# Second input ahead of the layer weights, and a reordered last stage, in a two-part attention and FFN kernel

## The chip, the cores and the metric

The kernel runs on one core of one Trainium2 chip. The metric is device time in microseconds (us), the median of three runs. The engines are named as in the profile: PE (TensorE; PEld its weight load), DVE (VectorE), ACT (ScalarE), POOL (GpSimd), SP (SyncE, whose queue issues every DMA here).

## What is computed

Eight sequences of 512 tokens with 256 features, all f32. Cut to its core:

```
xn = layernorm(x)                                  # over the features
s  = causal softmax attention(rotate(xn wq'), rotate(xn wk'), xn wv')
g  = xn
for l in range(2):                                 # two layers
    g = g + local_attention(shift(g) wqkv[l]) wo[l]        # 8 heads of 64, window 128
    h = layernorm(shift(g)) * ln_g[l] + ln_b[l]
    a, gate = split(h w1[l] + b1[l])                       # hidden width 682
    g = g + (a * gelu(gate)) w2[l] + b2[l]
out = x + s * silu(g)
```

`shift` delays the second half of the features by one token.

## The kernel before

Features lie on the partitions for the products, tokens for the softmax. Each f32 product is made of three fp32r products (high by high, high by low, low by high), so a value is split into a high part on ACT and a low part (the difference) on DVE or POOL.

**First block** (`attention_block`). It computes `xn` and `s`, batch by batch, in a software pipeline written out by hand: `step(0)` has only the front (transposes of x, projections, rotation), steps 1 to 7 have the front of one batch and the back (scores, softmax, values) of the one before, and step 8 only the back. Each engine has its own program of these steps, in order, tied by semaphores. SP first issues x of batch 0 (L289), the identity matrix and the three weights (one semaphore `w_in` for all, L293), the rotation tables and the mask (semaphore `c_in`, three DMAs, L294 to L296), and then everything that the second block wants for layer 0: `load_small` (31 small DMAs, L124 to L142), `wo` (L116), `w2` (L119, L120) and `wqkv` (L104). Only then comes `step(0)`, with x of batch 1 (L307), which waits until the normalized x of batch 0 is made (semaphore `xn`), for both use the one buffer `x_in`. POOL first multiplies the layers' tables by the scales of q and k (L324, semaphore `small`), then makes the rotation's second products (`t2`, L335 and L336). DVE waits for `c_in` at its start, before `statistics(0)` (L456). PE waits for all of `w_in` before it turns the weights (L568). In `step(0)` ACT runs `high`, `copy_x`, `proj(0)` (L348), `norm(1)` (it needs the statistics of batch 1), `proj(1)` and so on; DVE runs `low`, `statistics(1)`, `moments(1)`, `rotate(0)` (its sum is L485), `normal(1)` (L468), `rotate(1)` to `rotate(3)`.

**Second block** (`layers_block`). A pipeline over 16 (layer, batch) pairs: attention of pair i with the FFN of pair i-1. The last step, 16, has no attention (`if not attn`): it runs the FFN of the last batch, and the end of the kernel for all batches. The end of a batch is: PE turns a half of its features back to tokens (`turned_back(n)`, L1339, n = 2 b + half), ACT takes the silu of it (`silu(n)`, L921), and DVE multiplies by s and adds x (`combine(b)`, L1083 and L1085), after x and s of that batch have landed in `xs` (L786, 16 DMAs of 512 KB). SP then writes the batch out. Two PSUM banks take turns for n, so `turned_back(n)` waits for `silu(n-2)`. The FFN of the last batch goes: mean (L1241), difference (L1123), square on ACT (L945), sum of the squares on DVE (`sum_squares`, L1128), variance on PE (L1245), Ln and Exp on ACT (L949, L951), normalization on DVE (L1134), high part on ACT (`high_f`, L955), low part on DVE (L1145), first FFN product (`hidden`, L1260, 66 products), gelu on ACT (L903), `gated` (L1058) and `u_low` (L1067) on DVE, second FFN product (`down`, L1270, 18 products for each half of the features), `add_ffn` on DVE (L1073), and then the turns, silus and combines of batch 7.

ACT holds one table of functions at a time; `preload_act_table_set` loads one by name (L964 and L972 in this step).

Of the kernel before, what the change touches and what calls it, by code (L numbers as in the profile page):

```python
# [7 lines left out]
ALU = mybir.AluOpType  # L8
# [6 lines left out]
P = 128  # L15
B, N, D = 8, 512, 256
# [27 lines left out]
def at(ap, i):  # L44

    return ap[:, bass.ds(i, 1)]
# [158 lines left out]
def attention_block(nc, outer, io, W, xT, ident, identb, ones, epsc):  # L205
# [4 lines left out]
    with ctx:  # L210
# [6 lines left out]
        def sem(name):  # L217
# [41 lines left out]
        w_bank = (ring[0], ring[1], psT)  # L259
        qkT_bank = (psT, psP[0])  # L260

        names = ("id_in id_bf consts w_in c_in w_tr w_hi w_lo x_in0 bn agg lnv rstd xn xT_ps xT_hi xT_sb xT_lo "
                 "proj_ps proj_sb t2_done t1_done rot_done qkT_ps qkT_sb s_ps m_bias exp_done "
                 "rinv_done pT_ps pT_sb o_ps o_sb out_dma").split()
        S = {n: sem(n) for n in names}
# [7 lines left out]
        def pipeline(e, step):  # L273

            step(0, True, False)
            with e.Fori(1, B - 1) as i:
                step(i, True, True)
            step(B - 1, True, True)
            step(B, False, True)
# [7 lines left out]
        @block.sync  # L287
        def _(sp):
            sp.dma_start(x_in[:, :, :], x_v[0]).then_inc(S["x_in0"], 16)  # L289
            for j, w in enumerate(("wq", "wk", "wv")):  # L290
                if j == 0:
                    sp.dma_start(ident[:, :], io["ident"]).then_inc(S["id_in"], 16)
                sp.dma_start(wraw[:, KD * j:KD * (j + 1), :], io[w].rearrange("(k p) d -> p k d", p=P)).then_inc(S["w_in"], 16)  # L293
            sp.dma_start(cosT[:, :, :], io["acos"]).then_inc(S["c_in"], 16)  # L294
            sp.dma_start(sinT[:, :, :], io["asin"]).then_inc(S["c_in"], 16)
            sp.dma_start(maskT[:, :], io["amask"]).then_inc(S["c_in"], 16)  # L296
            W.load_small(sp, scl, scls)
            W.load_wo(sp, 0)
            sp.wait_ge(WS["w2pad"], 1)
            W.load_w2(sp, 0)  # L300
            sp.wait_ge(S["w_tr"], 3)
            W.load_wqkv(sp, 0, stage_q)

            def step(i, front, back):
                if has_next(i, front):
                    ge(sp, S["xn"], i + 1)
                    sp.dma_start(at(x_in[:, :, :].unsqueeze(1), 0), x_v[bass.ds(i + 1, 1)].rearrange("b p t d -> p b t d")).then_inc(S["x_in0"], 16)  # L307
                if back:
                    ge(sp, S["o_sb"], TT * i)
                    sp.dma_start(s_v[bass.ds(i - 1, 1)].rearrange("b p t d -> p b t d"), O[:, :, :].unsqueeze(1)).then_inc(S["out_dma"], 16)  # L310
                if isinstance(i, int) and i == B - 1:
                    W.load_w1(sp, 0, stage1)
            pipeline(sp, step)
            sp.wait_ge(S["out_dma"], 16 * (B + 1))

        @block.gpsimd
        def _(pool):
            pool.wait_ge(S["c_in"], 48)

            pool.wait_ge(WS["small"], W.SMALL)  # L320
            for l in range(LAYERS):
                for tab, s in ((W.cosT, scl), (W.sinT, scls)):
                    rows = tab[:, l].rearrange("p t j d -> p t (j d)")
                    pool.tensor_tensor(rows, rows, s[:, l].rearrange("p j d -> p (j d)").unsqueeze(1).broadcast_to([P, TT, 2 * DH]), ALU.mult).then_inc(WS["tabs"], 1)  # L324

            def step(i, front, back):
                if front:
                    for t in range(TT):

                        ge(pool, S["proj_sb"], TILES * i + t + 1)  # L330
                        ge(pool, S["rot_done"], TT * i + t - 1)
                        src = raw[:, t % 2, :].rearrange("p (q c s) -> p q c s", q=2, s=2)
                        dst = t2[:, t % 2, :].rearrange("p (q c s) -> p q c s", q=2, s=2)
                        tab = sinT[:, t, :].rearrange("p (c s) -> p c s", s=2).unsqueeze(1).broadcast_to([P, 2, D // 2, 2])
                        pool.tensor_tensor(dst[:, :, :, 0], src[:, :, :, 1], tab[:, :, :, 0], ALU.mult).then_inc(S["t2_done"], 1)  # L335
                        pool.tensor_tensor(dst[:, :, :, 1], src[:, :, :, 0], tab[:, :, :, 1], ALU.mult).then_inc(S["t2_done"], 1)  # L336
            pipeline(pool, step)

        @block.scalar
# [104 lines left out]
        def _(dve):  # L444
# [3 lines left out]
            dve.memset(W.b1raw[:, :, :], 0.0).then_inc(WS["b1pad"], 1)  # L448
            dve.memset(W.w2_raw[:, HFULL, :], 0.0).then_inc(WS["w2pad"], 1)
            dve.memset(spare[:, :], 0.0).then_inc(S["out_dma"], 16)  # L450
            dve.wait_ge(S["c_in"], 48)

            def statistics(i):
                ge(dve, S["x_in0"], 16 * (i + 1))
# [98 lines left out]
            for j in range(3):  # L553
                dve.wait_ge(S["w_hi"], j + 1)
                part = slice(j * D, (j + 1) * D)
                dve.scalar_tensor_tensor(out=wlo[:, :, part], in0=w_bank[j][:, :].rearrange("p (k o) -> p k o", k=KD), scalar=w_scale[j],
                                         in1=whi[:, :, part].bitcast(F32), op0=ALU.mult, op1=ALU.subtract).then_inc(S["w_lo"], 1)
            pipeline(dve, step)

        @block.tensor  # L560
        def _(pe):

            pe.wait_ge(S["id_in"], 16)
            pe.wait_ge(S["w_in"], 48)
            for j in range(3):
                for k in range(KD):
                    for o in range(KD):
                        last = pe.transpose(w_bank[j][:, k * D + o * P:k * D + (o + 1) * P],  # L568
                                            wraw[:, KD * j + o, k * P:(k + 1) * P], ident[:, :])
                last.then_inc(S["w_tr"], 1)  # L570
# [102 lines left out]
def layers_block(nc, outer, io, W, xT, ident, identb, ones, epsc):  # L673
# [3 lines left out]
    with ctx, stack:  # L677
# [184 lines left out]
        def _(act):  # L862
# [77 lines left out]
            def step(i, la, lf, last=False):  # L940
# [6 lines left out]
                def inverse_deviation():  # L947
                    ge(act, S["var_ps"], i)
                    act.activation(rstdF[:, :], psF[:, N:2 * N], ACT.Ln, bias=epsc[:, 0:1]).then_inc(S["lnF_done"], 1)  # L949
                    ge(act, S["lnF_done"], i)  # L950
                    act.activation(psF[:, 0:N], rstdF[:, :], ACT.Exp, scale=-0.5).then_inc(S["rstdF_done"], 1)  # L951
# [5 lines left out]
                if not attn:  # L957

                    act.preload_act_table_set(SILU)
                    for n in range(9):  # L960
                        silu(n)
                    square()
                    silu(9)
                    act.preload_act_table_set(NLE)  # L964
                    inverse_deviation()
                    high_f()
                    for j in range(HT):
                        gelu(i, j, lf, attn)
                        if j:
                            u_high(i, j - 1, attn)  # L970
                    u_high(i, HT - 1, attn)
                    act.preload_act_table_set(SILU)  # L972
                    for n in range(10, 2 * B):
                        silu(n)
                    return
                if attn:
# [46 lines left out]
        def _(dve):  # L1023
# [92 lines left out]
            def step(i, la, lf, last=False):  # L1116
# [20 lines left out]
                if not attn:  # L1137

                    less_mean()
                    combine(0)  # L1140
                    combine(1)
                    sum_squares()
                    normalize()
                    ge(dve, S["f_hi"], i)
                    dve.tensor_tensor(flo[:, :, :], dF, fhi[:, :, :].bitcast(F32), ALU.subtract).then_inc(S["f_lo"], 1)  # L1145
                    combine(2)
                    combine(3)
                    gated(i, 0, lf, attn)
                    combine(4)
                    for j in range(1, HT):  # L1150
                        gated(i, j, lf, attn)
                        u_low(i, j - 1, attn)
                    u_low(i, HT - 1, attn)
                    combine(5)
                    add_ffn(i, 0, lf)
                    combine(6)
                    combine(7, slice(0, 1))
                    add_ffn(i, 1, lf)
                    combine(7, slice(1, 2))
                    return  # L1160
# [61 lines left out]
        def _(pe):  # L1222
# [129 lines left out]
            def step(i, la, lf, last=False):  # L1352
                attn, ffn = la is not None, lf is not None
                turn = attn and ffn and la != lf
                if not attn:

                    for n in range(4):
                        turned_back(n)
                    mean(i)
                    for n in range(4, 9):  # L1360
                        turned_back(n)
                    variance(i)
                    turned_back(9)
                    for j in range(HT):
                        hidden(i, j, attn)
                    ge(pe, S["x_attn"], KD * i)
                    down(i, 0, range(HT))
                    for n in range(10, 14):
                        turned_back(n)
                    down(i, 1, range(0, 2))  # L1370
                    turned_back(14)
                    down(i, 1, range(2, HT))
                    turned_back(15)
                    return
                if turn:
# [131 lines left out]
```

## Time and profile before

| | |
|---|---|
| device time, median of 3 runs | 1488.77 us (1487.1 to 1489.69) |
| the profiled execution, device time | 1489.53 us |
| its span, first to last instruction | 1487.7 us |
| mean granted clock of PE | 0.98 of full speed |
| busy | PE 94%, DVE 65%, ACT 57%, POOL 51% |

The profiled execution has 1.83 us of device time outside its span, and is 0.76 us above the median. The table's shares are means over the span; the change touches only the first 50 us and the last 60 us.

### The profile page before, as it was taken

What the parts mean: (1) busy time and instruction counts of PE and PEld (TensorE: products, weight loads), DVE (VectorE), ACT (ScalarE), POOL (GpSimd) and SP (SyncE); (2) the same over time, 40 slices, a digit from 0 to 9 for tenths busy, and PEclk for the clock granted to TensorE, in tenths of its full rate; (3) what the DMA queues carried; (4) which work ended last, traced back from release to release, by engine and by line L of the source; (5) the groups of instructions that cost most, each with busy time, mean ns of one, the idle gap of its engine ahead of it and who ended that gap; (6) DMA issues with size and microseconds to landing.
All of it is one profiled execution on the core that took longest, in us unless ns stands there. A gap on an engine that the chain in (4) does not pass through costs nothing.

```text
span 1487.7 us, 24262 instructions
## 1 busy us (share of the span) xinstructions
PE 1399.3 (94%) x7828; PEld 1065.6 (72%) x7828; DVE 961.0 (65%) x2664; ACT 850.7 (57%) x2174; POOL 752.6 (51%) x514
## 2 busy tenths in 40 slices
PE   3999997899999999999999999999999999999967
PEld 2777775677777777777676767777777777777746
DVE  2676666576767676767676767666666666666646
ACT  1555554565656565656556564747474747474743
POOL 2342325374747474747474644747474747474700
PEclk9899998999999999999999999999999999999989
DMA  6101120000000000000001010000000000000064
GB/s 196 43 28 56 43 66 1 1 1 1 0 0 0 0 0 0 0 0 0 0 1 44 15 58 1 1 0 0 0 0 0 0 0 0 0 0 0 0 195 143
DMA packets 35239, 33.28 MB, mean 22 GB/s; under 512 B 8364, under 2 KB 32896, under 8 KB 35200
## 3 DMA queue, kind: packets, MB, share of 16 engines
q1 hardware_dynamic: 35200, 32.79, 6.9%
q8 instruction: 21, 0.34, 0.1%
q14 instruction: 18, 0.15, 0.0%
HBM read 24.39 MB, written 8.39 MB: 22 GB/s over the span
## 4 chain that ended last, share of the span: by engine, by line
PE 72%; ACT 6%; issue 3%; DVE 1%; POOL 1%; DMA 1%; ACTq 0%; SPq 0%; DVEq 0%; POOLq 0%
PE l_psF L1260 9%; PE l_ring L1234 9%; PE l_psP L1234 8%; PE l_ring L1260 7%; PE l_ring L1329 7%; PE l_psP L1313 7%; PE l_psF L1347 6%; PE l_psS L1270 4%; PE l_psS L1282 4%; ACT l_att L936 4%; PE l_psF L1299 4%; PE l_ring L1270 2%; PE l_psS L1299 2%; PE l_psF L1245 1%; PE l_psF L1241 1%
## 5 line engine op out<-in xcount | busy, mean ns | idle before, releaser
L805 POOL TENSOR_TENSOR l_att<-l_att 128x1024 f32<-128x1024 f32 x64 | 154.2, 2409 | 320.8 <-DVE l_att L1044 320.8
L852 POOL TENSOR_TENSOR l_att<-l_att,l_rinv 128x1024 f32<-128x1024 f32 x64 | 121.1, 1893 | 67.2 <-DVE l_rinv L1101 67.2
L821 POOL TENSOR_TENSOR l_u_lo<-l_att,l_u_hi 128x512 fp32r<-128x512 f32 x90 | 115.4, 1291 | 58.5 <-ACT l_u_hi L911 58.5
L916 ACT ACTIVATE l_att<-l_psP 128x384 f32<-128x384 f32 (+1 forms) x128 | 70.1, 548 | 130.5 <-PE l_psP L1313 130.5
L1106 DVE COPY l_att<-l_psP 128x384 f32<-128x384 f32 (+1 forms) x128 | 78.9, 616 | 83.7 <-PE l_psP L1313 81.7
L1313 PE MATMUL l_psP<-ident,l_att 128*128 128x128 f32 x896 | 125.8, 281 | 2.2 <-DVE l_att L1106 1.5
L1313 PEld LDWEIGHTS l_psP<-ident,l_att 128*128 128x128 f32 x896 | 99.7, 143 | 32.3 <-issue 30.1
L812 POOL TENSOR_TENSOR l_att<-l_att,l_rn 128x1024 f32<-128x1024 f32 x64 | 121.5, 1911 | 0.0
L936 ACT ACTIVATE l_att<-l_psF,l_nb 128x256 f32<-128x256 f32 x256 | 117.6, 483 | 0.0
L1094 DVE CUSTOM_DVE_ANT_0 l_psF<-l_psF,w_mask 128x256 f32<-128x256 f32 x256 | 101.2, 458 | 25.2 <-issue 25.2
L1329 PE MATMUL l_ring<-l_att 128*64 128x256 f32 (+1 forms) x1024 | 111.5, 360 | 1.4 <-ACT l_att L916 1.4
L936 ACT ACTIVATE l_att<-l_psS,l_nb 128x128 f32<-128x128 f32 (+1 forms) x256 | 104.5, 431 | 3.2 <-DVE l_nb L1094 2.8
L1329 PEld LDWEIGHTS l_ring<-l_att 128*64 128x64 f32 x1024 | 68.2, 137 | 51.7 <-issue 17.6
L1058 DVE SCALAR_TENSOR_TENSOR l_att<-l_psF,w_b,l_att 128x512 f32<-128x512 f32 x45 | 33.8, 751 | 108.3 <-ACT l_att L903 108.3
L1094 DVE CUSTOM_DVE_ANT_0 l_psS<-l_psS,w_mask 128x128 f32<-128x128 f32 (+1 forms) x256 | 83.6, 389 | 19.7 <-issue 19.5
L869 ACT ACTIVATE l_att<-l_ring 128x512 f32<-128x512 f32 x64 | 38.1, 595 | 96.6 <-PE l_ring L1234 96.6
L1234 PE MATMUL l_psP<-w_wq_hi,l_hhi 128*128 128x512 f32 x192 | 87.8, 457 | 0.0
L1260 PE MATMUL l_psF<-l_fhi,w_w_hi 128*128 128x512 f32 x192 | 80.7, 420 | 7.0 <-DVE l_flo L1145 7.0
L1234 PE MATMUL l_ring<-w_wq_hi,l_hhi 128*128 128x512 f32 x192 | 76.9, 401 | 7.3 <-POOL l_hlo L816 6.3
L335 POOL TENSOR_TENSOR a_t<-a_raw,a_tables 128x256 f32<-128x256 f32 x32 | 29.0, 907 | 107.7 <-ACT a_raw L348 107.7
L1299 PE MATMUL l_psF<-l_att 64*128 64x256 f32 x512 | 72.5, 402 | 9.5 <-ACT l_att L936 9.5
L1048 DVE TENSOR_REDUCE l_ssq<-l_att 128x16 f32<-128x1024 f32 x64 | 77.7, 1214 | 0.0
(202 smaller groups left out, 4064.4 us busy)
## 6 DMA issues: line engine op xcount, KB each, us to landing
a_tables<-in_x SPq DMA_DIRECT2D x8, 512.0 KB, 4.1
scratch_s<-a_o SPq DMA_DIRECT2D x8, 512.0 KB, 3.0
l_att<-in_x SPq DMA_DIRECT2D x8, 512.0 KB, 7.6
l_att<-scratch_s SPq DMA_DIRECT2D x8, 512.0 KB, 8.9
out_dram<-l_att SPq DMA_DIRECT2D x7, 512.0 KB, 5.1
aw_stage<-in_wqkv SPq DMA_DIRECT2D x2, 768.0 KB, 7.1
l_att<-in_wqkv SPq DMA_DIRECT2D x2, 768.0 KB, 5.4
w_w_raw<-in_w SPq DMA_DIRECT2D x2, 640.0 KB
```

The source lines that it names most:

```text
L805: pool.tensor_tensor(rot[:, t, :], rot[:, t, :], t2[t % 2], ALU.add).then_inc(S["added"], 1)
L812: pool.tensor_tensor(r, r, along(rn[:, t, :], DH), ALU.mult).then_inc(S["rot_done"], 1)
L821: pool.tensor_tensor(U_lo[0:rows, j, :], gate_of(j, attn)[0:rows, :], U_hi[0:rows, j, :].bitcast(F32), ALU.subtract).then_inc(S["u_lo"], 1)
L852: pool.tensor_tensor(pr, pr, along(inv, 2 * P), ALU.mult).then_inc(S["p_done"], 1)
L936: last = act.activation(Pr[u % 3][:, g * 2 * P + c0:(g + 1) * 2 * P], ps[:, g * 2 * P + c0:(g + 1) * 2 * P], ACT.Exp, bias=nb[:, u % 3, g: ...
L1094: last = dve.tensor_tensor_reduce(out=block, in0=block, in1=maskT[:, c0:2 * P], scale=1.0, scalar=3e38, op0=ALU.add, op1=ALU.min, accum_ou ...
L1234: last = pe.matmul(proj_of[(3 * t + c) % 4], a[:, k, t * P:(t + 1) * P], w[:, k, c * INNER:(c + 1) * INNER], start=(m == 0), stop=(m == 3 ...
L1260: last = pe.matmul(hidden_of[j % 2][bank], w[:, k, tile * P:(tile + 1) * P], a[:, k, :], start=(m == 0), stop=(m == 3 * KD - 1))
L1270: last = pe.matmul(down_of[c], w[:, k, c * P:(c + 1) * P], u[:, k, :], start=(k == 0 and m == 0), stop=(k == HT - 1 and m == 2))
L1299: last = pe.matmul(ps[:, par * 512 + tt * 2 * P + c0:par * 512 + (tt + 1) * 2 * P], QT[rows, pair, t * P:(t + 1) * P], KT[rows, pair, max( ...
L1313: last = pe.transpose(psP[:, dst:dst + P], Pr[u % 3][:, src:src + P], ident[:, :])
L1329: last = pe.matmul(ring[pair % 2][rows, t * P:t * P + w], V[:, t, h * DH:(h + 1) * DH], PT[:, par, t * 2 * P:t * 2 * P + w], start=(t == 0 ...
```

## The change

1. First block, start. SP issues x of batch 1 (in `step(0)`) ahead of the layer weights, which follow in `layer_weights()`. POOL's products on the layers' tables move from its start to its last step (`layer_tables()`). DVE's wait for `c_in` moves behind the statistics and normalization of batch 0 and the splitting of the weights. PE waits for each of the three weights by itself.
2. Last step, normalization. `sum_squares` comes before `combine(1)` on DVE, and `turned_back(9)` before the variance on PE.
3. Last step, turns. `turned_back(10)` to `(13)` and their silus come before the first FFN product instead of between the two halves of the second. For this ACT loads the table of silu once more, ahead of `high_f`. `combine(5)` moves in between the gated products, and three tiles of the second half of `down` instead of two come before `turned_back(14)`.

```
             sp.dma_start(maskT[:, :], io["amask"]).then_inc(S["c_in"], 16)
-            W.load_small(sp, scl, scls)
-            W.load_wo(sp, 0)
-            sp.wait_ge(WS["w2pad"], 1)
-            W.load_w2(sp, 0)
-            sp.wait_ge(S["w_tr"], 3)
-            W.load_wqkv(sp, 0, stage_q)
+            def layer_weights():
+                W.load_small(sp, scl, scls)
+                W.load_wo(sp, 0)
+                sp.wait_ge(WS["w2pad"], 1)
+                W.load_w2(sp, 0)
+                sp.wait_ge(S["w_tr"], 3)
+                W.load_wqkv(sp, 0, stage_q)
             def step(i, front, back):
                 if has_next(i, front):
                     ge(sp, S["xn"], i + 1)
                     sp.dma_start(... x of batch i + 1 ...)
+                if not back:
+                    layer_weights()
...
         def _(pool):
             pool.wait_ge(S["c_in"], 48)
-            pool.wait_ge(WS["small"], W.SMALL)
-            for l in range(LAYERS):
...
             def step(i, front, back):
...
+                else:
+                    layer_tables()
...
             dve.memset(spare[:, :], 0.0).then_inc(S["out_dma"], 16)
-            dve.wait_ge(S["c_in"], 48)
...
+            dve.wait_ge(S["c_in"], 48)
             pipeline(dve, step)
...
-            pe.wait_ge(S["w_in"], 48)
             for j in range(3):
+                pe.wait_ge(S[f"w_in{j}"], 16)
...
                     inverse_deviation()
+                    act.preload_act_table_set(SILU)
                     high_f()
+                    for n in range(10, 14):
+                        silu(n)
                     for j in range(HT):
                         gelu(i, j, lf, attn)
...
                     act.preload_act_table_set(SILU)
-                    for n in range(10, 2 * B):
+                    for n in range(14, 2 * B):
                         silu(n)
...
                     combine(0)
+                    sum_squares()
                     combine(1)
-                    sum_squares()
                     normalize()
...
                     for j in range(1, HT):
                         gated(i, j, lf, attn)
                         u_low(i, j - 1, attn)
+                        if j == 3:
+                            combine(5)
                     u_low(i, HT - 1, attn)
-                    combine(5)
                     add_ffn(i, 0, lf)
...
-                    for n in range(4, 9):
+                    for n in range(4, 10):
                         turned_back(n)
                     variance(i)
-                    turned_back(9)
+                    for n in range(10, 14):
+                        turned_back(n)
                     for j in range(HT):
                         hidden(i, j, attn)
                     ge(pe, S["x_attn"], KD * i)
                     down(i, 0, range(HT))
-                    for n in range(10, 14):
-                        turned_back(n)
-                    down(i, 1, range(0, 2))
+                    down(i, 1, range(0, 3))
                     turned_back(14)
-                    down(i, 1, range(2, HT))
+                    down(i, 1, range(3, HT))
                     turned_back(15)
```

## Rows read from the trace of the kernel before

**Rows 1.** Page, the chain that ended last: shares of the span by engine.

```profile
PE 72%; ACT 6%; issue 3%; DVE 1%; POOL 1%; DMA 1%; ACTq 0%; SPq 0%; DVEq 0%; POOLq 0%
```

**Rows 2.** Waits, first 60 us: who waited for what, us, times, longest.

```profile
POOL w_cos L324 <- DMA w_b1raw<-in_b: 23.7, 1, 23.7
...
PE a_ring L593 <- ACT a_raw L348: 8.8, 1, 8.8
PE a_ring L568 <- DMA aw_stage<-in_wv: 7.7, 1, 7.7
```

**Rows 3.** Timeline, first 55 us: start, us, engine, line, idle before.

```profile
4.81 0.45 SPq L124 DMA_DIRECT2D w_mask<-in_fmask  x1
...
10.92 1.41 DVE L456 BATCH_NORM_STATS2 a_stats<-a_tables 128x6 f32<-128x256 f32 x4 [9.55 <-DMA a_mask<-in_amask]
...
16.82 1.94 PE L579 MATMUL a_ring<-ident,a_xn 128*128 128x128 f32 x8 [6.30 <-DVE aw_lo L556]
...
24.47 0.60 ACT L348 ACTIVATE a_raw<-a_ring 128x512 f32<-128x512 f32 x1 [3.65 <-PE a_ring L593]
...
24.68 15.96 SPq L307 DMA_DIRECT2D a_tables<-in_x  x2
...
29.14 0.83 POOL L335 TENSOR_TENSOR a_t<-a_raw,a_tables 128x256 f32<-128x256 f32 x1
...
33.50 1.41 DVE L456 BATCH_NORM_STATS2 a_stats<-a_tables 128x6 f32<-128x256 f32 x4 [12.12 <-DMA a_tables<-in_x]
...
35.94 0.69 DVE L485 TENSOR_TENSOR a_rot<-a_rot,a_t 128x512 f32<-128x512 f32 x1
...
47.56 1.29 PE L579 MATMUL a_ring<-ident,a_xn 128*128 128x128 f32 x8
...
54.10 1.39 DVE L456 BATCH_NORM_STATS2 a_stats<-a_tables 128x6 f32<-128x256 f32 x4
```

**Rows 4.** Page, DMA issues: count, KB each, median us from issue to landing.

```profile
a_tables<-in_x SPq DMA_DIRECT2D x8, 512.0 KB, 4.1
```

**Rows 5.** The chain that ended last, from 1428 us: start, us, what.

```profile
1429.55 8.81 DMA l_att<-scratch_s
...
1441.59 2.07 PE l_psF L1245 x2
1443.66 0.87 PE l_psS L1339 x4
...
1445.17 1.28 ACT L964
...
1447.82 1.30 DVE l_ffn L1134 x2
...
1451.50 4.79 PE l_psF L1260 x12
1456.30 2.80 PE l_ring L1260 x12
...
1468.89 4.21 PE l_ring L1270 x18
...
1473.57 1.10 ACT xT L921 x2
...
1481.48 0.75 DVE xT L1073
```

**Rows 6.** Timeline of DVE, ACT and SP, 1428 to 1440 us.

```profile
1433.16 1.23 DVE L1083 TENSOR_TENSOR xT<-xT,l_att 128x1024 f32<-128x1024 f32 x1 [0.29 <-DMA l_att<-scratch_s]
...
1435.25 1.05 ACT L945 ACTIVATE l_ffn<-l_ffn 128x1024 f32<-128x1024 f32 x1
...
1438.65 1.42 SPq L786 DMA_DIRECT2D l_att<-scratch_s  x1
```

**Rows 7.** Windows of the last step: us, busy (instructions) of PE, PEld, DVE, ACT, POOL, PEclk, DMA share, GB/s.

```profile
1438.00:1439.00 1.00, 0.00 (x0) 0.00 (x0) 0.55 (x1) 0.00 (x0) 0.00 (x0) 0.63 1.09 352
1455.00:1468.70 13.70, 13.70 (x59) 11.00 (x58) 8.74 (x11) 5.48 (x9) 0.00 (x0) 0.99 0.45 158
```

More of the change, by code:

```diff
@@ L260, in attention_block @@
         qkT_bank = (psT, psP[0])
-        names = ("id_in id_bf consts w_in c_in w_tr w_hi w_lo x_in0 bn agg lnv rstd xn xT_ps xT_hi xT_sb xT_lo "
+        names = ("id_in id_bf consts w_in0 w_in1 w_in2 c_in w_tr w_hi w_lo x_in0 bn agg lnv rstd xn xT_ps xT_hi xT_sb xT_lo "
                  "proj_ps proj_sb t2_done t1_done rot_done qkT_ps qkT_sb s_ps m_bias exp_done "
@@ L292, in _ @@
                     sp.dma_start(ident[:, :], io["ident"]).then_inc(S["id_in"], 16)
-                sp.dma_start(wraw[:, KD * j:KD * (j + 1), :], io[w].rearrange("(k p) d -> p k d", p=P)).then_inc(S["w_in"], 16)
+                sp.dma_start(wraw[:, KD * j:KD * (j + 1), :], io[w].rearrange("(k p) d -> p k d", p=P)).then_inc(S[f"w_in{j}"], 16)
             sp.dma_start(cosT[:, :, :], io["acos"]).then_inc(S["c_in"], 16)
@@ L318, in _, with layer_tables @@
             pool.wait_ge(S["c_in"], 48)
-            pool.wait_ge(WS["small"], W.SMALL)
-            for l in range(LAYERS):
-                for tab, s in ((W.cosT, scl), (W.sinT, scls)):
-                    rows = tab[:, l].rearrange("p t j d -> p t (j d)")
-                    pool.tensor_tensor(rows, rows, s[:, l].rearrange("p j d -> p (j d)").unsqueeze(1).broadcast_to([P, TT, 2 * DH]), ALU.mult).then_inc(WS["tabs"], 1)
+            def layer_tables():
+                pool.wait_ge(WS["small"], W.SMALL)
+                for l in range(LAYERS):
+                    for tab, s in ((W.cosT, scl), (W.sinT, scls)):
+                        rows = tab[:, l].rearrange("p t j d -> p t (j d)")
+                        pool.tensor_tensor(rows, rows, s[:, l].rearrange("p j d -> p (j d)").unsqueeze(1).broadcast_to([P, TT, 2 * DH]), ALU.mult).then_inc(WS["tabs"], 1)
             def step(i, front, back):
```

## The prediction

> **What bounds the kernel now.** I began with the chain that ended last: 72% of it is PE [rows 1], so over most of the kernel only PE's work counts, and nothing of it is touched. The change can pay only where PE stands still, so I read the waits and the timeline of the first 55 us, then the chain and the windows of the last 60 us.
>
> At the start the reader is to see four late things [rows 2, 3]. PE turns the first weights at 7.7 us, when the third of them has landed. DVE begins the statistics of batch 0 at 10.92, held for 9.55 us by the mask, which they don't use. PE's product L593 waits 8.8 us for ACT's copy of the second projection; ACT runs `norm(1)` ahead of that copy, and `norm(1)` wants batch 1's statistics, which start at 33.50, when x of batch 1 lands; SP came to issue it at 24.68, behind 19.87 us of issuing layer loads (4.81 to 24.68). And POOL waits 23.7 us for the last small load, so that its first rotation product comes at 29.14.
>
> At the end: batch 0's x and s have landed at 1433.16, and batch 1's s only 8.81 us after its issue at 1429.55, at 1438.4 [rows 5, 6]. `combine(1)` waits for them with `sum_squares` behind it, and behind that stand variance, normalization and all FFN products. The square was ready at 1436.3 (1435.25 + 1.05).
>
> **The change, part 1: the start.** The steps, each against the rows of before:
> - x of batch 0 is SP's first issue, in the first microsecond. With a typical landing 4.1 us later [rows 4] the statistics start at about 4.85. From there to PE's `x_transposes(0)` DVE's serial work took 5.90 us (10.92 to 16.82) [rows 3], so that comes at 10.75, not 16.82. The weights need not hold it: they land by 7.7, and separate semaphores can only let PE start earlier. If they did hold it, it would be by about 1 us: I take nothing, and keep 1 us for the range.
> - ACT's copy of projection 0 shifts by the same 6.07 us, from 24.47 to 18.40, and ends at 19.0. POOL is free now, since its table products have gone; its two rotation products take 0.83 us each, to 20.7, up to 0.4 more if they collide with DVE's; I take 0.3. DVE's sum (0.69 us) ends at about 21.65. Before it ended at 36.63 (35.94 + 0.69) [rows 3]. That is 15.0 us earlier. The product and wait that were there before, statistics of batch 1, don't hold it: normalized x of batch 0 exists at 8.7, x of batch 1 is issued then, lands after the rotation tables and the mask (10.9), so by about 12.5, and is wanted after `low(0)` at about 15.
> - From that sum to `x_transposes(1)` at 47.56 it took 10.9 us of rotations on DVE and POOL, and that order is unchanged. So step 1 begins at about 32.6, 15.0 us earlier. PE's clock adds both ways: before, the products of this stretch ran partly at the low clock after the 8.8 us of standing still; now the standing still is gone, but shorter gaps stay. I allow 0.3 more and 1.7 less, and take 14.8.
> - What moves behind: the layer loads, all 36 DMAs of them, now start at about 9.1 and hold SP's queue for the same 19.87 us, to 29.0. Behind them stands x of batch 2. Before, x of batch 1 stood behind the same loads and landed 8.8 us after its issue (24.68 to 33.50). So batch 2's lands at 37.8. It is wanted 6.5 us into step 1 (47.56 to 54.10), that is at 39.1. Hidden, with only 1.3 us to spare. The later users of SP's queue (s of batch 0, x of batch 3) come well behind.
> - POOL's four products on the tables, some 5 us (four between 24.2 and 29.1), move to its last step, where it has nothing else. Their cover is the whole back of step 8; without it they would cost up to 5 us. I take nothing.
>
> **Part 2: sum of squares ahead of batch 1.** DVE can do it when the square is ready, 1436.3, and is done at 1437.0. PE stood still only since 1435.2, and the windows show its clock granted in full until it falls within 1438 to 1439 [rows 7]; the two variance instructions took 2.07 us at the low clock [rows 5], so about 1.1 now, to 1438.15. Ln and Exp (1446.46 to 1447.8 before, 1.35 us) end at 1439.5. So `normalize` now waits for `combine(1)` alone, which runs 1438.45 to 1440.93: it starts at 1440.95 where it started at 1447.82 [rows 5]. That is 6.87 us, and the new bound is the landing of batch 1, which nothing moves.
>
> The added table load is 1.28 us (L964) [rows 5], and would lie from 1439.5 to 1440.8, under `combine(1)`; `high_f` isn't wanted before 1442.25. Hidden, with 1.4 us to spare. The Trainium skill (ScalarE: Activation LUTs, What ACT_TABLE_LOAD costs) speaks against it: it says that each switch of tables costs a drain of some 1.38 us besides a load of 1283 ns. Here the load's row agrees with its 1.28, and Ln follows 0.01 us behind it, with no drain to be seen; by the page's price two switches would put `high_f` off by about 1.4 us, and the sum would be 1.4 less.
>
> **Part 3: turns ahead of the first FFN product.** From `normalize` to the first product was 3.68 us (1447.82 to 1451.50) [rows 5]. Now PE must first turn n = 12 and 13, which want silu 10 and 11, and those stand behind `high_f` (1442.25 to 1443.3): they end at 1443.9 and 1444.4 (two took 1.10 us). PE, cold after standing still from about 1439, turns each half in 0.87 us at the low clock [rows 5]: 1443.98 to 1445.7. So the products begin at 1445.7, not at the 1444.65 at which the low part is ready: this costs 1.05 us here, and what the four turns and their waits took later comes back (below).
>
> The first 12 products took 4.79 us, later ones 2.80 [rows 5]: about 3.6 us of low clock. In it PE now does 1.74 us of turning, so the 66 products take 17.23 - 0.87 = 16.4 us and end at 1462.1, not at 1468.73: 6.6 us gained. If the clock is never low here, they begin at 1444.9 and end at 1460.3 (8.4 gained); if the low stretch takes as long again, 3.6 us more, 4.8.
>
> Does DVE keep up? In 13.7 us of the product stretch it was busy 8.74 [rows 7], with `combine(3)`, so there is room for one more combine (2.46 us, two of 1.23 [rows 6]). `combine(2)` and `(3)` now lie before the first gated product, `combine(5)` in front of the fifth: 2.5 us of work in a rhythm of 2.80 us makes gated 4 late by 1.1 us, and the last low parts of u, which `down` wants tile by tile, by about 0.9. The `down` half of 4.21 us [rows 5] then waits about 0.4 us in all.
>
> From the end of the 66 products to `add_ffn(1)` it was 12.75 us (1468.73 to 1481.48). Now: 4.2 + 0.4, three tiles 2.1, one turn 0.45, three tiles 2.1, and 0.4 of pipeline at the ends: 9.65. The gain is 3.1 us: `combine(5)` no longer stands in front of `add_ffn(0)`, and the four turns are gone. What follows `add_ffn(1)`, the last turn, silu, combine and write, is unchanged at 6.2 us. I take 6.5 + 3.0 = 9.5 us for the end.
>
> **Sum.** 14.8 + 9.5 = 24.3 us. The profiled execution has 1489.53, so 1465.2; against the median, 0.76 lower, 1464.5. Where I rounded, I leaned on neither side; I say 1465.
>
> **Rivals.**
> - *x of batch 2 lands late.* For: 1.3 us of spare, at the end of a queue of 36. Against: the same loads ran without a stop before. Each us late is a us in step 1. With 4 us late, 1468.5.
> - *The clock takes back.* PE restarts cold at both places. A low stretch twice as long at the end (1.8 us) and up to 2.5 us lost in steps 0 and 1 give 1469. For: the clock moved with standing still at every such place.
> - *The end gains little.* The two orders trade one wait for another: if batch 2, 3 or 4 land late, `combine(2)` to `(4)` hold the gated products. Transfers moved 350 GB/s [rows 7], 3.0 us for a batch's 1.05 MB: batches 2, 3, 4 at 1441.4, 1444.4, 1447.4, wanted at 1444.5, 1447, 1450.8. For it speaks only that batch 1 took longer than this. All of part 3 lost: 1469.5.
> - *The table load shows.* If a switch costs more than its row, or `high_f` needs yet another load of 1.28 us, more than the spare 1.4 is used, and the chain behind `high_f` shifts by up to 1.4: 1466.4. The trace has no such gap; this is the page's rule as a mechanism of this kernel.
> - *Slower.* SP's issuing slows while x of batch 1 is in flight. Near 0.55 us per load here (19.87 for 36); with 1.42, as an issue at the end took behind other large loads [rows 6], SP is free at 60 us, x of batch 2 lands at 69, 30 us late: 1471 to 1495. It decides from about 1.25 us per issue on. Against: small loads, and only one large one ahead of them.
> - *Nothing at the start.* If the layer weights, not x, were what step 0 wants; excluded almost, as their first user is step 8.
>
> **How the numbers follow.** Forecast as summed, within 1461 to 1468: 0.63. The table load shows: 0.03. x of batch 2 late: 0.09. Clock: 0.13. End gains little: 0.07. Slower or near it: 0.03, and others 0.02. The range, 1460.5 to 1470.5, takes in the best clock at the end (1.9 more), 1.1 more at the start, and the rivals up to all of part 3 lost. What this measurement can tell from no change is 0.2%, 3 us. Faster by more 0.97, within 0.01, slower 0.02.
>
> **What would show it.** In the profile after: statistics of batch 0 at 4.9 us, of batch 1 at 15; `x_transposes(1)` at 32.6; no wait of DVE for x of batch 2 at 39; `sum_squares` ahead of `combine(1)`, right behind the square; `normalize` 2.5 us behind batch 1's landing; the first FFN product 4.75 us behind `normalize`; a 0.4 us wait in `down`. What would make me wrong above all: a wait of DVE for x in step 1, and PE's speed in steps 0 and 1.

## The result

| | us |
|---|---|
| before, median of 4 runs | 1488.72 (1487.1 to 1489.69) |
| after, median of 4 runs | 1465.34 (1464.07 to 1466.3) |
| ratio | 0.9844, 95% interval 0.9826 to 0.9861 |
| span of the profiled execution, before and after | 1487.7, 1464.4 |

The change makes the kernel 23.4 us (1.6%) faster. The forecast was 1465.0, within 1460.5 to 1470.5. Each experiment below is compared with runs of the kernel before that were taken beside it.

The start, in the timeline of the kernel after (lines as in [rows 3]; L462, L586, L355, L491, L309 are what L456, L579, L348, L485, L307 were):

```profile
4.27 1.40 DVE L462 BATCH_NORM_STATS2 a_stats<-a_tables 128x6 f32<-128x256 f32 x4 [2.90 <-DMA a_tables<-in_x]
...
6.85 1.94 PE L575 MATMUL a_ring<-ident,aw_stage 128*128 128x128 f32 x8 [6.85 <-DMA aw_stage<-in_wq]
...
8.16 0.38 SPq L309 DMA_DIRECT2D a_tables<-in_x  x1
...
11.10 1.94 PE L586 MATMUL a_ring<-ident,a_xn 128*128 128x128 f32 x8 [1.46 <-issue]
...
18.79 0.60 ACT L355 ACTIVATE a_raw<-a_ring 128x512 f32<-128x512 f32 x1 [3.65 <-PE a_ring L600]
...
21.73 1.26 DVE L491 TENSOR_TENSOR a_rot<-a_rot,a_t 128x512 f32<-128x512 f32 x1 [1.62 <-POOL a_t L341]
...
27.93 0.40 SPq L309 DMA_DIRECT2D a_tables<-in_x  x1
...
33.83 1.29 PE L586 MATMUL a_ring<-ident,a_xn 128*128 128x128 f32 x8
...
40.37 1.39 DVE L462 BATCH_NORM_STATS2 a_stats<-a_tables 128x6 f32<-128x256 f32 x4
```

Statistics start at 4.27 instead of 10.92, x of batch 1 is issued at 8.16 instead of 24.68, and step 1 (the second L586) begins at 33.83 instead of 47.56 [rows 3]: 13.73 us. The last line has no wait: x of batch 2, issued at 27.93 behind the loads, was there in time.

The last step, in the chain that ended last of the kernel after (as [rows 5]):

```profile
1416.40 7.92 DMA l_att<-scratch_s
...
1424.41 1.24 DVE xT L1093
...
1426.81 1.29 DVE l_ffn L1144 x2
...
1428.12 1.06 ACT l_fhi L962
...
1429.81 1.09 PE l_psP L1350 x4
1430.90 0.85 PE l_psS L1350 x4
1431.75 4.44 PE l_psF L1271 x12
1436.19 2.80 PE l_ring L1271 x12
...
1451.66 1.75 PE l_ring L1281 x6
...
1458.09 0.76 DVE xT L1083
```

The transfer of batch 1's s (7.92 us from issue to landing) is still at the head of it, but `normalize` (L1144) now begins 2.40 us behind `combine(1)` (L1093), where 9.4 us lay between them before (1438.45 to 1447.82). Two turns (L1350) stand in front of the first FFN product. The granted clock (the last figure but two) in that stretch, in windows (columns as in [rows 7]):

```profile
1430.00:1435.00 5.00, 5.00 (x17) 4.23 (x17) 4.93 (x5) 2.63 (x4) 0.00 (x0) 0.50 1.11 351
1435.00:1448.60 13.60, 13.60 (x59) 10.98 (x58) 9.15 (x12) 5.50 (x9) 0.00 (x0) 0.99 0.99 336
```

All times of the table below are read from the timeline of one execution of each kernel. "Last step" is the issue of its first load (L786 before; 1428.03 and 1414.88 us); the columns right of it count from there. "66 products" is how long the first FFN product took, from its start to the start of the second.

| run | x transposes 0 | step 1 | last step | normalize | first product | 66 products | `add_ffn(1)` | end of span |
|---|---|---|---|---|---|---|---|---|
| before | 16.82 | 47.56 | 1428.03 | 19.79 | 23.47 | 17.23 | 53.45 | 59.67 |
| after | 11.10 | 33.83 | 1414.88 | 11.93 | 16.52 | 17.23 | 43.21 | 49.52 |
| start_only | 10.34 | 31.66 | 1412.56 | 19.39 | 23.08 | 17.29 | 53.11 | 59.44 |
| end_only | 16.61 | 47.64 | 1429.53 | 12.19 | 16.78 | 17.18 | 43.41 | 49.67 |
| squares_only | 16.30 | 47.45 | 1428.36 | 12.31 | 15.99 | 17.43 | 46.16 | 52.44 |
| turns_only | 16.59 | 47.29 | 1429.56 | 19.47 | 24.07 | 16.86 | 50.39 | 56.64 |
| waits_only | 10.62 | 47.79 | 1428.76 | 18.11 | 21.79 | 17.86 | 52.39 | 58.64 |
| queue_only | 16.51 | 38.60 | 1419.33 | 19.16 | 22.84 | 17.24 | 52.82 | 59.07 |
| tables_stay | 10.04 | 44.76 | 1425.13 | 17.79 | 21.48 | 18.06 | 52.28 | 58.57 |
| late_loads | 10.51 | 31.78 | 1426.55 | 11.90 | 16.50 | 17.03 | 42.98 | 49.25 |
| two_more_loads | 10.37 | 33.14 | 1414.08 | 11.76 | 18.69 | 16.32 | 44.47 | 50.72 |
| apart | 10.84 | 34.80 | 1414.86 | 12.51 | 17.10 | 16.31 | 42.87 | 49.14 |
| earlier_square | 10.18 | 32.56 | 1413.49 | 9.58 | 15.58 | 16.12 | 41.14 | 47.41 |
| square_apart | 10.67 | 33.24 | 1414.13 | 9.57 | 15.57 | 16.18 | 41.22 | 47.47 |

### The profile page after: what moved, and what is told of

It reads as the page before. It is cut to its first block, busy times and chain, and to the rows that moved or that the text cites. A ratio compares the mean times of both kernels' runs of the same rounds, so it can differ in the third digit from the quotient of the medians.

```text
span 1464.4 us, 24262 instructions
## 1 busy us (share of the span) xinstructions
PE 1397.7 (95%) x7828; PEld 1066.0 (73%) x7828; DVE 961.4 (66%) x2664; ACT 853.1 (58%) x2175; POOL 754.2 (52%) x514
## 4 chain that ended last, share of the span: by engine, by line
PE 72%; ACT 6%; issue 3%; DVE 1%; POOL 1%; DMA 1%; ACTq 0%; SPq 0%; DVEq 0%; POOLq 0%
PE l_psF L1271 9%; PE l_ring L1245 9%; PE l_psP L1245 9%; PE l_ring L1271 7%; PE l_ring L1340 7%; PE l_psP L1324 7%; PE l_psF L1358 6%; PE l_psS L1281 5%; ACT l_att L943 4%; PE l_psS L1293 4%; PE l_psF L1310 4%; PE l_ring L1281 2%; PE l_psS L1310 2%; PE l_psF L1252 1%; PE l_psF L1256 1%
```

## The experiments

Theory: the gain is two separate sums, 13 to 15 us at the start (x of batch 1 and POOL's hands free) and 9 to 10 at the end (normalization ahead, then the turns). Rivals: they overlap or give something back; x of batch 2 lands late; the table load has a price beyond its row; the clock takes back.

**1. start_only**: the diff's hunks in `attention_block` alone.

> Part 1 of the change alone (queue order, tables to POOL's last step, the mask's and the weights' waits). My theory: the two parts touch separate stretches and add up. The trace of the full change has step 1's x transposes at 33.83 us where before had 47.56, and 13.15 us are left of that when the last step begins. So 13 to 14 us faster than before, about 1475.3. Rival: what is gained at the start is partly given back later; then the last step begins less than 12 us earlier and the time is above 1477.

1475.28 us, ratio 0.9906 (0.9891 to 0.9921): 14.3 us by the medians. In its timeline step 1 came 15.9 us earlier and the last step 15.5: what the start gains is kept to the end. (The profiled execution, 1473.75 us, was the fastest of the four.)

**2. end_only**: the hunks in `layers_block` alone.

> Parts 2 and 3 alone, the start as before. From the first load of the last step to the end the full change took 49.52 us where before took 59.67: 10.15 us faster, about 1478.6. Rival: a part of the gain came from the shifted start (transfers that met other work); then less than 9.

1480.51 us, ratio 0.9931 (0.9918 to 0.9945), beside 1489.57 for before: 9.1 us by the medians, 10.3 by the ratio; the last step took 49.67 us against 59.67. With 1, the ratios make 0.9906 x 0.9931 = 0.9838, and the whole had 0.9844 (0.9826 to 0.9861): they add up.

**3. squares_only**:

```
                     combine(0)
+                    sum_squares()
                     combine(1)
-                    sum_squares()
...
-                    for n in range(4, 9):
+                    for n in range(4, 10):
                         turned_back(n)
                     variance(i)
-                    turned_back(9)
```

> Part 2 alone: sum of squares ahead of batch 1's products, turn 9 ahead of the variance. My theory: normalization then waits for batch 1's products and its data alone, 6.9 us earlier, and nothing behind it changes: 6.9 us faster (6 to 8, as batch 1's data came 0.9 us sooner in the full change), 1481.8. Rival: the clock of TensorE, which stands still longer ahead of the first FFN product, takes back up to 2 us: 1484.

1482.65 us, ratio 0.9955 (0.9941 to 0.9968): 6.7 us. Normalization came 7.5 us earlier and the end 7.2: nearly nothing was given back to the clock (the 66 products took 0.2 us longer).

**4. turns_only**: part 3 without part 2 (turns, silus and table load ahead, `combine(5)` in between).

> Part 3 alone: four turns and their silus ahead of the first FFN product, products of batch 5 in between the gated ones. My theory: it costs about 1 us ahead of the first FFN product and gives 3.3 back behind it (12.75 against 9.46 us from its end to the last addition of the FFN): 2.3 us faster, 1486.4. Rival: without part 2 the turns stand in the way and the two cancel: within 1 us of before. The added table load has only 0.04 us of cover here; if it costs a drain of its own besides its 1.28 us, the gain falls to about 1.

1486.47 us, ratio 0.9979 (0.9969 to 0.9989): 3.1 us. The first product stood 4.60 us behind normalization, where it was 3.68 before: 0.9 us lost. The 66 products took 0.4 us less, and from their end to `add_ffn(1)` it was 9.46 us for 12.75: 3.3 us won. The table load had 0.04 us of cover, and no drain showed (it began at 1449.02 and took 1.28 us, the high part began at 1450.35).

**5. waits_only**: DVE's wait for `c_in` moved and one semaphore per weight, the queue and POOL as before.

> Of part 1 only the waits: DVE's wait for tables and mask behind its first work, one semaphore per weight. Queue and POOL as before. My theory: batch 0's x transposes come 5.7 us earlier (at 11.1), but x of batch 1 is still issued at 24.7 and lands at 33.5, so step 1 begins where it did: 0 to 0.5 us. Rival: the earlier start of batch 0 is worth something by itself: 2 us or more.

1488.95 beside 1488.58 us, ratio 1.0001 (0.9992 to 1.0011). Batch 0 is early and stands still: in its timeline, DVE waits for x of batch 1 longer (18.36 us for 12.12) by what it has gained (6.2).

```profile
33.57 1.41 DVE L455 BATCH_NORM_STATS2 a_stats<-a_tables 128x6 f32<-128x256 f32 x4 [18.36 <-DMA a_tables<-in_x]
```

**6. queue_only**: `layer_weights()` and `layer_tables()` as in the change, `c_in` and `w_in` as before.

> Of part 1 only the order of the queue and POOL's tables; DVE waits for the mask as before. My theory: x transposes of batch 0 at 16.8 as before, and from there to step 1's the same 22.7 us as in the full change (11.10 to 33.83): step 1 at 39.6, 8 us faster, 1480.7. Rival: the whole gain is the queue's (over 12 us).

1481.09 us, ratio 0.9953 (0.9936 to 0.9970); step 1 at 38.60, 9.0 us earlier. The waits that were worth nothing alone (5) are worth 5 to 7 more us on top of it.

**7. tables_stay**: part 1 but for POOL, which keeps the four table products and their wait for `small` at its start.

> Part 1 with POOL's products on the layers' tables left at its start. They wait for the last small load, which is now issued 3 to 4 us later than before. My theory: POOL's first rotation product at about 32 us, its sum on DVE at 34 to 35, step 1 at 45: 2 to 3 us faster only, so that moving POOL's tables carries 11 of the 13.7 us. Rival: DVE and PE don't need POOL that early: over 8 us faster.

1486.42 us, ratio 0.9986 (0.9977 to 0.9996); step 1 at 44.76. In its timeline POOL is held by the wait for the last small load:

```profile
26.61 1.26 POOL L328 TENSOR_TENSOR w_cos<-w_cos,a_scl 128x512 f32<-128x512 f32 x1 [26.16 <-DMA w_b1raw<-in_b]
...
31.49 0.83 POOL L339 TENSOR_TENSOR a_t<-a_raw,a_tables 128x256 f32<-128x256 f32 x1
```

ACT began its copy of projection 0 at 16.84 (0.60 us long), and POOL used it 14.6 us behind that. So the line that looks like tidying carries 11 to 13 us of the start: all the rest of part 1 is worth 2.8 us at step 1 as long as POOL waits for what was put behind x.

**8. late_loads**:

```
                 if not back:
+                    sp.wait_ge(S["xn"], 2)
                     layer_weights()
```

> The full change, with the layer loads held in the queue until batch 1 is normalized (25.9 us), so that x of batch 2 lands late behind them. Loads take 19.0 us to issue, x of batch 2 is issued at about 45.2 and lands 4 to 9 us later, 49 to 54, and DVE wants it at 40.4: a wait of 9 to 14 us in step 1, and the time 9 to 14 us above the full change, 1474 to 1479. That shows what stands behind the queue. Rival: step 1 has slack and less than half of the lateness is seen.

1478.91 us, 13.6 above the full change. In its timeline, x of batch 2 is issued at 43.72 and DVE waits for it:

```profile
43.72 0.40 SPq L309 DMA_DIRECT2D a_tables<-in_x  x1
52.18 1.40 DVE L463 BATCH_NORM_STATS2 a_stats<-a_tables 128x6 f32<-128x256 f32 x4 [13.76 <-DMA a_tables<-in_x]
```

DVE's wait of 13.8 us is the 13.6 us of time: once x is later than DVE wants it, step 1 has no slack. In the full change x was issued at 27.93 and took 8.8 us to land (the profile's DMA view), so it was there at 36.7, and it was wanted at 40.37: 3.6 us to spare. The same reading gives 1.5 us in 1 (issue 27.96, 8.7 us to land, wanted at 38.19) and 1.3 in 9 (28.21, 10.2, 39.67).

**9. two_more_loads**: `preload_act_table_set(NLE)` and `(SILU)` once more ahead of `high_f`.

> The full change with two more table loads (to the logarithm's table and back to silu's) behind the one that was added. In the full change the added load ended at 1427.71 and the high part began at 1428.12: 0.41 us of cover. My theory: a load costs its own 1.28 us and no drain: three in a row take 3.84 us, the high part comes 2.15 us later, and the kernel is 2.1 us slower than the full change. Rival (a drain of some 1.38 us with each): 2.8 us more, some 5 us slower.

1466.63 us, 1.3 above the full change. ACT's timeline:

```profile
1425.00 0.60 ACT L958 ACTIVATE l_psF<-l_ffn 128x512 f32<-128x512 f32 x1
1425.62 1.28 ACT L973 ACT_TABLE_LOAD   x1
1426.91 1.28 ACT L974 ACT_TABLE_LOAD   x1
1428.20 1.28 ACT L975 ACT_TABLE_LOAD   x1
1429.49 1.06 ACT L962 ACTIVATE l_fhi<-l_ffn 128x1024 fp32r<-128x1024 f32 x1
```

Three loads stand 1.29 us apart, with no drain. The first product came 2.17 us later, as forecast, but `add_ffn(1)` only 1.26, for the 66 products took 16.32 us and not 17.23; the expectation of 2.1 missed by 0.8. Whether the delay itself shortened them isn't shown: in 10, whose last step has the code of the full change, they took 16.31. The chain's first 12 of them, in 9, in 10 and in the full change:

```profile
1433.12 3.53 PE l_psF L1273 x12
...
1432.31 3.52 PE l_psF L1274 x12
...
1431.75 4.44 PE l_psF L1271 x12
```

That there is no drain rests on ACT's rows, not on the time: 1.3 us is close to what the stretch of the 66 products differs by from run to run (16.31 to 17.23 us with the same code).

**10. apart**:

```
-                        ge(pool, S["rot_done"], TT * i + t - 1)
+                        if isinstance(i, int) and i == 0 and t:
+                            pool.wait_ge(S["rot_done"], t)
+                        else:
+                            ge(pool, S["rot_done"], TT * i + t - 1)
```

> The full change; in step 0 POOL begins its products of tile t only when DVE's sum of tile t-1 is done, so that the two don't run together. In the full change that first sum took 1.26 us instead of 0.69 beside POOL. My theory: the sum takes 0.69 us again and step 1's x transposes come 0.3 to 0.6 us earlier than 33.83. Rival: POOL, started later, becomes the last of the chain and step 1 comes later, up to 1 us.

1465.83 us, ratio 0.9847 (0.9834 to 0.9861), as the full change. The theory fell, and the rival's 1 us came. DVE's timeline: the first sum took 0.69 us again, but two of the next three waited for POOL, and step 1 came at 34.80.

```profile
21.46 0.69 DVE L494 TENSOR_TENSOR a_rot<-a_rot,a_t 128x512 f32<-128x512 f32 x1 [1.62 <-POOL a_t L344]
...
28.06 0.69 DVE L494 TENSOR_TENSOR a_rot<-a_rot,a_t 128x512 f32<-128x512 f32 x1 [1.61 <-POOL a_t L344]
```

**11. earlier_square**, an improvement that follows from 3: the square on ACT behind silu 5, then silus 6 and 7 and the logarithm's table; silus 8 to 13 behind `high_f`; `combine(1)` behind the low part.

```
-                    combine(0)
                     sum_squares()
-                    combine(1)
+                    combine(0)
                     normalize()
```

> The full change, taken further: the square comes on ACT behind silu 5 instead of 8, sum of squares ahead of batch 0's products, table load behind silu 7, and normalization no longer waits for batch 1's products; silus 8 to 13 come behind the high part. My theory: normalization begins 2.2 us earlier (Ln at 8.3 instead of 10.2 us behind the first load of the last step), PE turns 10 to 13 cold behind it, and warms up earlier: the first FFN product ends 1.0 to 1.6 us earlier, and so does the kernel, 1464. Rival: six silus behind the high part, two at a time with PE, hold the first FFN product as late as before: no change or up to 1 us slower.

1462.72 us, ratio 0.9827 (0.9814 to 0.9841). It beats both kernels: 2.6 us below the full change by the medians, with its slowest run (1463.49) below the fastest of the full change (1464.07); 2.1 by the length of the last step (47.41 against 49.52, and 49.14 to 49.67 over all runs with the full change's last step but 9). Normalization came 2.35 us earlier, as expected, and no longer waits for a transfer. The first product came 0.94 us earlier. The 66 products took 16.12 us (16.18 in 12) for 17.23; PE had been turning since 12.6 us into the step, which fits, but 10 had 16.31 without it, so this 1.1 us is not shown to come from the turns. ACT's timeline shows that the added load has 0.06 us of cover, and that nothing more than its 1.28 us appears (the high part begins 1.32 us behind `normalize`, as it did before the change with no load there, 1.31):

```profile
1422.44 0.60 ACT L958 ACTIVATE l_psF<-l_ffn 128x512 f32<-128x512 f32 x1
1423.05 1.28 ACT L974 ACT_TABLE_LOAD   x1
1424.39 1.06 ACT L962 ACTIVATE l_fhi<-l_ffn 128x1024 fp32r<-128x1024 f32 x1
```

**12. square_apart**: 11, with the wait of 10 for tile 1 alone.

> The kernel with the earlier square, and in step 0 only tile 1's products on POOL wait for DVE's sum of tile 0. With all tiles waiting, the sum took 0.69 us as expected, but DVE then waited 1.6 us for POOL at tiles 2 and 3, and step 1 came 23.96 us behind batch 0's x transposes, where the full change had 22.73 and the one with the change's start alone, in which the two did not meet, 21.32. My theory: with the one wait the sum takes 0.69 us, tiles 2 and 3 don't wait longer than before, and the stretch takes 21.3 to 22.2 us; the kernel gains 0.5 to 1 us on the one with the earlier square. Rival: the stretch depends on the clock of TensorE, not on the meeting: 22.4 or more, no gain.

1462.99 us, ratio 0.9827 (0.9814 to 0.9841), no gain on 11. The sum took 0.69 us, and the stretch between the two x transposes 22.57. In 11 the sum happened to take 0.69 us without the wait, and the stretch was 22.38; with the meeting it was 22.73 in the full change. The meeting of POOL and DVE isn't what makes it long.

## Why the prediction was right

Point by point, with its own steps:

- *Start, batch 0.* x landed at 4.27, not 4.85; the weights, put down at nothing, did hold it. The first landed at 6.85, ACT's splits came 0.86 us apart behind PE's turns, and DVE's serial work of 5.90 us took 6.83. The 1 us kept for the range was right; x transposes at 11.10 for 10.75. It depends on the run: in 1 the first weight landed at 5.99, and the work took 5.91 us behind x.
- *To DVE's sum.* It began at 21.73, not 20.96: ACT's copy came at 18.79 for 18.40, and POOL's two products took 2.1 us beside DVE's, for 1.96 with the allowance.
- *To step 1.* From the sum's start 12.10 us, for 11.6. Together 33.83 for 32.55: the term of 14.8 us measured 13.7 here. Its size varies with the run: five kernels with the same start (the full change, 1, 8, 9 and 11) have step 1 at 31.66 to 33.83, 13.7 to 15.9 us earlier than before, 15.0 in the mean. The forecast lies in the middle, and the execution profiled after the change was the latest of the five. Between the first and last sums of step 0 lay 8.89 us in the full change, 8.83 in 1 and 8.96 in 12, so the meeting of POOL and DVE costs nothing. What differs is ahead (9.74 us from x transposes to the first sum in 1 and 8, 10.6 in the others) and behind (2.75 in 1, 3.21 in the full change). Ahead it is PE's: in 1 and 8 the first x transposes show as 1.07 and 1.06 us for eight, where the full change took 1.94. The granted clock doesn't tell them apart, for its row shows 1.00 from 10 to 12 us in both, so the cause stays open. Behind, the granted clock was 0.82 in 1 (28.91 to 31.66) and 0.73 in the full change (30.62 to 33.83), which fits, but was not tested.
- *x of batch 2.* Hidden, as forecast. The spare was 3.6 us, not 1.3: the loads began 0.5 us sooner and took 19.3 us (8.59 to 27.93) instead of 19.87, and step 1 came 1.3 later. In 1 and 9 it was 1.5 and 1.3, so the small margin was real. SP's issuing didn't slow.
- *Tables at POOL's last step.* Hidden, as forecast, and worth far more than "it is free now" said: 7 shows it.
- *Between the stages.* 13.73 us at step 1 had become 13.15 at the last step. The loss of 0.6 us isn't explained; in 1 it was 0.4.
- *Sum of squares.* 7.86 us (19.79 to 11.93), for 6.87: the bound is batch 1's landing, as said, and that came 0.9 us sooner. The runs have it 8.4 to 10.4 us into the step. (The prediction has PE standing still since 1435.2; the row of its wait before the variance puts it at 1434.7. The sum doesn't need it.) Behind this bound stands another, close by: the log table's load, which the prediction passes over (1423.65 to 1424.93), and the variance let Exp end at 1426.41, 0.40 us before `normalize` began. In 10 the variance took 2.08 us at the low clock instead of 1.12, and `normalize`, 12.51 us into the step, waited 0.66 us for Exp and not for the transfer. That the variance runs at full speed, as the prediction has it, isn't sure.
- *The table load.* 0.41 us of cover was left of 1.4, since batch 1 came sooner: the high part was wanted 13.2 us into the step instead of 14.2, and the load ended where it was forecast, at 12.8. The Trainium skill (ScalarE: Activation LUTs, What ACT_TABLE_LOAD costs) gives a drain of some 1.38 us with each load; 4, 9 and 11 show 1.28 to 1.29 us and nothing else. By the page's price (an estimate from its figure) the two further loads of 9 would have held the high part some 2.8 us longer than its row does. The measurement decides.
- *Turns.* They held the first product 0.97 us behind the low part, for 1.05. But the low clock lasted from the first turn to about 1435.1, 5.3 us and not 3.6: the 66 products took 17.23 us, for 16.4, exactly as long as before the change. The 0.87 us that the turns were to save by filling the low clock is the term that failed; the lower case of the range (4.8 us gained up to there, not 6.6) covers it. It isn't a fixed loss: with the same last step the products took 17.18 us in 2, 17.03 in 8 and 16.31 in 10. At this place the state of the clock differs from run to run: while PE stood between 1428 and 1430 us, 0.50 was granted in the full change and 1.00 in 10.
- *Behind the products.* 9.46 us to `add_ffn(1)` (1448.63 to 1458.09), for 9.65; the wait in `down` was 0.23 us (1451.43 to 1451.66), for 0.4. Of the 3.3 us gained against before, its timeline puts 2.26 on the four turns (1472.93 to 1475.19) and 1.06 on turn 14's wait for DVE, which had `combine(5)` in front of `add_ffn(0)`; no run separates the two.

The end in all: 10.15 us for 9.5; normalization gave 7.9, the turns took 0.9 in front of the products, nothing in them, and gave 3.3 behind. The start, as far as the last step sees it: 13.15 for 14.8. The mechanism was right in both. That 23.3 us came out for 24.3 is partly luck: the errors went opposite ways, and the terms differ from run to run by more than that (13.7 to 15.9 us at step 1, 16.3 to 17.2 us for the 66 products).

## What to carry to other kernels

Waits in a row are not worth their sum one by one. The earlier waits gave nothing alone (5), the queue 7 us (6), both 14 (1); ask of each freed step what it waits for next, and of everything put further back in a queue who waits for it at the head of another. Work that must be done anyway is best taken out of the tail, where each turn waits for a silu: the four turns, with `combine(5)`, cost 0.9 us ahead of the products and gave 3.3 behind them. Don't count on such work to fill the low clock: here the products behind it took as long as before.

## What the runs showed of the hardware

- Three table loads in a row took 1.28 us each and began 1.29 us apart, and the next instruction followed 0.01 us behind them (9).
- A stretch that begins at the low clock differs in length from run to run with the same code: 16.31 to 17.23 us for the 66 products. A delay of 2.17 us in front of them reached the end as 1.26 (9). In 5 and 7 batch 1's s came 1.7 and 2.0 us sooner than in before, and the products took 0.6 and 0.8 us longer. Both look as if such a stretch takes up a part of a shift; no run separates this from the scatter.
- At the start the clock's row and PE's pace disagree: in the full change the row shows 1.00 from 16 to 18 us, with products 0.43 us apart, and 0.50 from 1432 to 1434, with the same products the same 0.43 us apart. There the pace has to be read from the instructions.
- Loads that land behind others vary by 2 us over the kernels, where DVE's wait shows the landing: batch 1's came 8.4 (tables_stay) to 10.4 us (before) into the last step, with the same loads in front of them in that step.
